# A graph layer's attention scores on VectorE: 16 multiply-and-add operations per sub-batch in place of two products and one sum

## The chip, the cores and the metric

The kernel runs on one core of one Trainium2 chip. The metric is the device time of one execution in microseconds (us); smaller is better. The kernel before takes 2039.41 us, the median of three runs (2039.25 to 2039.56).

A core has TensorE (PE, with its weight loads shown as PEld), VectorE (DVE), ScalarE (ACT), GpSimd (POOL) and SyncE (SP), which work side by side, each through its own instructions in order, and meet at semaphores.

## The reference

A graph of 6250 nodes with 256 features has 100000 edges of 5 types. Each node gets a query, a key and a value per type, each of 4 heads of 64 elements. An edge's score is the dot product of its target's query and its source's key, head by head; the scores are normalized by a softmax over the edges that share target and type, and weigh the values that are added up in the target node.

```python
q_i = Q[edge_type, dst]
k_j = K[edge_type, src]
v_j = V[edge_type, src]
score = jnp.sum(q_i * k_j, axis=-1) * scale          # per edge and head, over 64 elements
seg = dst * R + edge_type
m = jax.ops.segment_max(score, seg, num_segments=N * R)
e = jnp.exp(score - m[seg])
s = jax.ops.segment_sum(e, seg, num_segments=N * R)
alpha = e / s[seg]
out = jax.ops.segment_sum(v_j * alpha[..., None], dst, num_segments=N)
x = _layernorm(x + out.reshape(N, HD) + bias, axis=-1)
```

## The kernel before

The kernel has three stages. In the first, VectorE sorts the edges by target and type while TensorE makes queries, keys and values of all nodes, which go to tables in DRAM. The second stage walks over the sorted edges. The third adds the input, normalizes and stores. The change lies in the second stage alone.

In the second stage 128 edges form a tile (one edge per partition), 4 tiles a sub-batch (`SB = 4`), 8 sub-batches a batch of 32 tiles for which the softmax is done at once (`PERC = 8`). There are 208 sub-batches (`NSB`). All engines run a loop over the sub-batch number `s`, each with its own program, and nothing orders them but semaphores. For one sub-batch:

- GpSimd starts 4 gathers (line 468), one per tile: for each edge the row of its source's value and key (2 x 256 f32) goes from DRAM into the ring `ring_v`/`ring_k`, which has 22 places. Before a gather it waits on `s_mul` for the scores of the sub-batch 5 earlier, and on `s_agg` for the ring's place.
- SyncE loads the queries' rows of the sub-batch (line 532) and, broadcast, their places (`rel_tab`, line 525).
- TensorE (`lift`, line 709) spreads the queries to the edges with a one-hot matrix: four tiles of 128x256 into two PSUM banks, `qk`, in two halves of two tiles. Each half waits on `s_mul` until VectorE has read that half of the sub-batch before, and signals `s_lift`. Then `aggregate` (line 697) adds up the weighted values of the sub-batch 13 back.
- ScalarE scales values by their weights (line 881) and moves finished windows into the accumulator `acc` (line 899).
- VectorE runs the loop over `s` that is quoted below. `products(s, half)` (line 1210) multiplies two tiles of keys in SBUF by two tiles of queries in PSUM: 128x512 elements into `prod`. `scores(s)` (line 1216) adds up `prod` over the 64 elements of each tile and head: 128x1024 elements into 16 columns of `sc`. Around them stand four small additions of columns to the accumulator, `add_first` (line 1293, each waits for the one before through `s_acc`), the weighting of one tile of values (`payload`, line 1276), the one-hot matrix for the queries (line 1199) and four one-hot matrices for the aggregation (line 1267). In four of eight sub-batches `weights_a` and `weights_b` add a part of the softmax: running maxima and sums (lines 1220 to 1227), differences and a reciprocal (line 1259).

```python
                if s < NSB:
                    products(s, 0)
                if adds:
                    dve.wait_ge(s_cols, q - 1)
                    add_first(q - 2, 0, at)
                if s < NSB:
                    products(s, 1)
                ...
                if s < NSB:
                    scores(s)
```

Of the kernel before, what the change touches and what calls it, by code (L numbers as in the profile page):

```python
# [8 lines left out]
def gnn_kernel(nc, x, src, dst, etype, Wq, bq, Wk, bk, Wv, bv, bias, out):  # L9
    f32, i32, u16, bf16 = mybir.dt.float32, mybir.dt.int32, mybir.dt.uint16, mybir.dt.bfloat16  # L10
    ALU, ACT, AX = mybir.AluOpType, mybir.ActivationFunctionType, mybir.AxisListType
# [4 lines left out]
    H = 4  # L16
    D = C // H
# [33 lines left out]
    SB = 4  # L51
    NSB = TT // SB
    PERC = G // SB
# [92 lines left out]
    with ctx:  # L146
# [88 lines left out]
        ring_k = ring_v[:, C:C + RING].rearrange("p (i l c) -> p i l c", i=SB, l=KS)  # L235
# [5 lines left out]
        sc = cut(2 * H * G).rearrange("p (s h g) -> p s h g", s=2, h=H)  # L241
# [16 lines left out]
        prod = cut(SB * C).rearrange("p (i w) -> p i w", i=SB)  # L258
# [25 lines left out]
        qk = pairs.rearrange("p b (i w) -> p (b i) w", w=C)  # L284
# [27 lines left out]
        s_oht, s_lift, s_mul, s_sc = sem("s_oht"), sem("s_lifted"), sem("s_mul"), sem("s_sc")  # L312
# [48 lines left out]
        def spot(s):  # L361

            return KSTEP * s % KS
# [193 lines left out]
        def _(pe):  # L557
# [58 lines left out]
            for o in range(NO):  # L616
# [15 lines left out]
                for k in range(KC):  # L632
                    done = nc.tensor.matmul(bank[o % 4][0:n, 0:w], acc[:, k, t * P:t * P + n],  # L633
                                            w_sb[:, k, :, :].rearrange("p u c -> p (u c)")[:, c0:c0 + w],
                                            start=(k == 0 and o >= OA), stop=(k == KC - 1))
# [39 lines left out]
            def weights_b(s):  # L675
                c, k = piece(s)
                if k == 0:
                    pe.wait_ge(s_sc, s + 1)
                    nc.tensor.transpose(bank[6][:, 0:P], sc[:, c % 2, :, :].rearrange("p h g -> p (h g)"), ident[:]  # L679
                                        ).then_inc(s_ST, 1)  # L680
                if k == 1:
                    turn_carries(c, 0)
                if k == 2:
                    turn_rows(c, 1)
# [43 lines left out]
            for u, t in enumerate((recM, recD, recS)):  # L728
                done = nc.tensor.transpose(bank[6][0:64, u * P:(u + 1) * P], t[:].rearrange("p s c -> p (s c)"), ident[:])
            done.then_inc(s_r1, 1)  # L730
            pe.wait_ge(s_r2, 1)
            for h in range(H):
                done = nc.tensor.transpose(bank[7][0:64, h * 64:(h + 1) * 64],
                                           M4[0:64, h:h + 1].broadcast_to([64, 64]), ident[0:64, 0:64])
# [4 lines left out]
            for half in range(2):  # L739
                done = nc.tensor.transpose(bank[5][0:64, half * P:(half + 1) * P],  # L740
                                           recT[:, half, :, :].rearrange("p s c -> p (s c)"), ident[:])
# [3 lines left out]
            for half in range(2):  # L745
                done = nc.tensor.transpose(bank[6][:, half * 64:(half + 1) * 64], recV[0:64, half * P:(half + 1) * P],
                                           ident[0:64, 0:64])
# [205 lines left out]
        def _(dve):  # L953
# [21 lines left out]
                                                op0=ALU.mult, op1=ALU.add))  # L975
# [226 lines left out]
            def products(s, half):  # L1202

                if half == 0:
                    dve.wait_ge(s_got[s % KL], gathered(s))
                dve.wait_ge(s_lift, 2 * s + half + 1)
                if s > 0:
                    dve.wait_ge(s_sc, s)
                two = slice(2 * half, 2 * half + 2)
                nc.vector.tensor_tensor(prod[:, two, :], ring_k[:, two, spot(s), :], qk[:, two, :], ALU.mult  # L1210
                                        ).then_inc(s_mul, 1)

            def scores(s):
                dve.wait_ge(s_mul, 2 * s + 2)
                g = SB * (s % PERC)
                nc.vector.tensor_reduce(sc[:, (s // PERC) % 2, :, g:g + SB].rearrange("p h g -> p g h"),  # L1216
                                        prod.rearrange("p i (h d) -> p i h d", h=H), AX.X, ALU.add).then_inc(s_sc, 1)

            def scans(to, data, flags, op, start):
                c.go(nc.vector.tensor_tensor_scan(to[:, 0, :], flags[:, 0:P], data[:], start[0], op[0], op[1]))  # L1220
# [79 lines left out]
            for s in range(NSB + LAG + 2):  # L1300
                u, q = s - AHEAD, s - LAG
                adds = 0 <= q - 2 < NSB
                if adds and q % 2 == 0:
                    at = load_nodes(q - 2)
# [8 lines that stand above are left out]
                    add_first(q - 2, 1, at)  # L1313
                weights_a(s)
                if adds:
                    add_first(q - 2, 2, at)
                if s < NSB:
                    scores(s)
                if 0 <= u < NSB:
                    payload(u)  # L1320
                if s + 2 < NSB:
                    turned_one_hot(s + 2)
                if adds:
                    add_first(q - 2, 3, at)
                if 0 <= q + 1 < NSB:
                    one_hot(q + 1)
                if adds and (q - 2) % PERC == PERC - 1:
                    sum_records((q - 2) // PERC)
                weights_b(s)
# [109 lines left out]
```

## Time and profile before

| | |
|---|---|
| median of three runs | 2039.41 us |
| the profiled execution | 2043.67 us, its span 2041.9 us |
| busy over the span | PE 1692.2 us (83%), DVE 1619.3 us (79%), POOL 1152.7 us (56%), ACT 1045.8 us (51%) |
| line 1210, products | 416 instructions, 278.3 us |
| line 1216, sums of products | 208 instructions, 252.1 us |

The page's part on slices cuts the span into 40 equal pieces and gives each engine's busy share in tenths. A row of the timeline has the start of an instruction in us from the start of the span, its duration in us, the engine, line and operation, output and inputs, and in brackets how long the engine stood idle before and what ended that. Durations on VectorE overlap: an instruction's record lasts until its results are written, and the next one often starts before that. So two figures are told apart here, the record (the duration of a row) and the pitch (from a row's start to the start of the next one on the engine), and where VectorE never stands idle the pitches are what adds up to time. Rows of several instructions (x2, x4) run from the first's start to the last's end.

### The profile page before, as it was taken

The page shows a single profiled execution, that of the slowest core. Times are in us where ns is not written, and L with a number is a line of the kernel's source. Part 1 is how long each engine was busy: PE and PEld are TensorE (multiplying, and loading weights), DVE is VectorE, ACT ScalarE, POOL GpSimd, SP SyncE. Part 2 cuts the span into 40 slices and gives each one's busy share as a digit, 9 for nine tenths or more (in the row PEclk, how much of TensorE's full clock was granted, in tenths as well). Part 3 has the DMA queues.
Part 4 walks back from the last instruction along what each step waited for, and adds up shares of the span by engine and source line. Part 5 has one row for each costly group of instructions (what it writes and reads, how often), then busy time and mean ns, then how long its engine had stood idle before and what let it go on. Part 6 is the DMA issues. An engine that isn't in the chain of part 4 may idle for free.

```text
span 2041.9 us, 33205 instructions
## 1 busy us (share of the span) xinstructions
PE 1692.2 (83%) x7565; PEld 1136.7 (56%) x7565; DVE 1619.3 (79%) x4151; ACT 1045.8 (51%) x4107; POOL 1152.7 (56%) x1215
## 2 busy tenths in 40 slices
PE   5999999999999995687788877788777887788645
PEld 2444444444444443466666666666666676677534
DVE  7988897454443344799999999999999999999548
ACT  1223330200000000378888788788888888878835
POOL 2000005777777505777777777777777777776105
PEclk9999999999999997899999999999999999989668
DMA  6333344999999948999999999999999999998006
GB/s 214 124 124 109 124 141 160 313 350 364 364 362 363 339 154 292 339 318 329 320 316 320 318 333 311 320 320 321 334 309 321 320 326 329 324 306 291 24 22 210
DMA packets 339496, 555.34 MB, mean 272 GB/s; under 512 B 44045, under 2 KB 238831, under 8 KB 339298
## 3 DMA queue, kind: packets, MB, share of 16 engines
q0 software_dynamic: 80880, 256.60, 36.7%
q1 hardware_dynamic: 222180, 228.67, 34.2%
q10 hardware_dynamic: 36238, 67.94, 9.2%
q8 instruction: 61, 1.00, 0.2%
q14 instruction: 137, 1.12, 0.2%
HBM read 412.09 MB, written 140.94 MB: 271 GB/s over the span
## 4 chain that ended last, share of the span: by engine, by line
DVE 35%; PE 33%; issue 16%; POOL 8%; DMA 4%; DVEq 2%; ACT 1%; SPq 0%; ACTq 0%; POOLq 0%
PE sums L633 24%; POOL region L468 8%; DVE region L996 6%; DVE region L1267 5%; DVE region L1210 4%; PE pairs L709 4%; DVE region L1199 3%; PE sums L697 3%; DMA region<-kv_tab,kvidx 3%; DVE acc L1293 3%; DVE region L1276 2%; DVEq L1284 1%; DVE region L1221 1%; DVE region L1400 1%; DVE region L1403 1%
## 5 line engine op out<-in xcount | busy, mean ns | idle before, releaser
L468 POOL DMA_INDIRECT region<-kv_tab,kvidx x831 | 818.2, 985 | 361.1 <-issue 214.8
L881 ACT ACTIVATE region<-region 128x64 f32<-128x64 f32 x2496 | 694.1, 351 | 0.0
L633 PE MATMUL sums<-region,acc 128*128 128x512 f32 (+2 forms) x1568 | 679.5, 579 | 4.1 <-DVE region L1171 3.3
L709 PE MATMUL pairs<-region 128*128 128x256 f32 x1664 | 449.4, 416 | 181.7 <-DVE region L1210 156.4
L709 PEld LDWEIGHTS pairs<-region 128*128 128x128 f32 x1664 | 323.3, 204 | 256.6 <-issue 195.1
L697 PE MATMUL sums<-region 128*128 128x131 f32 x3328 | 438.5, 286 | 28.1 <-issue 24.5
L633 PEld LDWEIGHTS sums<-region,acc 128*128 128x128 f32 (+1 forms) x1568 | 284.8, 190 | 305.9 <-issue 290.4
L697 PEld LDWEIGHTS sums<-region 128*128 128x128 f32 x3328 | 417.1, 199 | 60.2 <-issue 52.2
L1177 DVE TENSOR_TENSOR region<-sums,region 128x512 f32<-128x512 f32 (+1 forms) x245 | 168.7, 690 | 249.9 <-PE sums L633 245.5
L450 POOL DMA_INDIRECT region<-q_tab,region x288 | 275.3, 956 | 92.8 <-issue 61.3
L899 ACT COPY acc<-sums 128x256 f32 x832 | 305.9, 368 | 30.0 <-PE sums L697 28.6
L1210 DVE TENSOR_TENSOR region<-region,pairs 128x512 f32<-128x512 f32 x416 | 278.3, 675 | 36.5 <-DMA region<-kv_tab,kvidx 24.5
L1216 DVE TENSOR_REDUCE region<-region 128x16 f32<-128x1024 f32 x208 | 252.1, 1212 | 0.8 <-issue 0.2
L868 ACT COPY region<-bank 128x128 f32<-128x128 f32 x26 | 6.9, 266 | 424.6 <-PE bank L679 423.8
L1267 DVE TENSOR_SCALAR region<-iota_f,nrel 128x131 f32<-128x131 f32 x832 | 195.1, 311 | 12.8 <-PE sums L697 12.8
L996 DVE TENSOR_TENSOR region<-region 128x512 f32<-128x512 f32 x292 | 188.9, 688 | 5.1
L787 ACT COPY region<-sums 128x512 f32<-128x512 f32 x138 | 71.1, 515 | 210.6 <-PE sums L633 210.6
L1293 DVE TENSOR_TENSOR acc<-acc,region 128x2 f32 x832 | 129.4, 156 | 30.8 <-ACT region L907 10.1
L430 POOL DMA_DIRECT2D rel_tab<-region x1 | 0.8, 768 | 245.7 <-DVE region L1113 245.7
L1199 DVE TENSOR_SCALAR region<-region,part_f 128x512 f32<-128x512 bf16 x208 | 101.6, 488 | 11.2 <-DMA region<-rel_tab 11.2
L477 POOL TENSOR_TENSOR region<-region 128x256 f32<-128x256 f32 (+1 forms) x49 | 35.4, 734 | 113.8 <-DMA region<-in_x 113.6
L1276 DVE TENSOR_TENSOR region<-region 128x256 f32<-128x256 f32 x208 | 86.4, 415 | 0.0
(246 smaller groups left out, 953.0 us busy)
## 6 DMA issues: line engine op xcount, KB each, us to landing
region<-q_seg SPq DMA_DIRECT2D x832, 128.0 KB
kv_tab<-region ACTq DMA_DIRECT2D x48, 1280.0 KB, 7.7
q_seg<-region SPq DMA_DIRECT2D x288, 128.0 KB, 5.3
q_tab<-region SPq DMA_DIRECT2D x48, 640.0 KB, 3.3
region<-rel_tab SPq DMA_DIRECT2D x208, 128.0 KB, 5.2
region<-kv_tab,kvidx POOLq DMA_INDIRECT x831
region<-in_x SPq DMA_DIRECT2D x96, 128.0 KB, 3.1
out<-region SPq DMA_DIRECT2D x48, 128.0 KB, 2.3
```

Source lines behind the costliest of these rows:

```text
L450: pool.indirect_dma_start(pq[:, j % PQ, :], None, q_tab, bass.IndirectOffsetOnAxis(ap=seg_list[:, j:j + 1], axis=0)).then_inc(s_pq[j % PQ] ...
L468: pool.indirect_dma_start(ring_row[:, a:a + 2 * C], None, kv_tab, bass.IndirectOffsetOnAxis(ap=kvidx[:, t:t + 1], axis=0)).then_inc(s_got[ ...
L633: done = nc.tensor.matmul(bank[o % 4][0:n, 0:w], acc[:, k, t * P:t * P + n], w_sb[:, k, :, :].rearrange("p u c -> p (u c)")[:, c0:c0 + w], ...
L697: done = nc.tensor.matmul(bank[i][:, h * W:(h + 1) * W], ring_v[:, i, spot(q), h * P:(h + 1) * P], oneh[:, q % 2, i, :], start=True, stop= ...
L709: done = nc.tensor.matmul(qk[:, i, :], oht[:, s % 2, i * P:(i + 1) * P], qring[:, s % QS, i, :], start=True, stop=True)
L881: done = nc.scalar.activation(ring_v[:, i, spot(q), h * D:(h + 1) * D], ring_v[:, i, spot(q), h * D:(h + 1) * D], ACT.Copy, scale=alT[:, h ...
L899: nc.scalar.copy(acc[:, :, bass.ds(at[(q % 2) * SB + i] + 1, P)], bank[i][:, 0:2 * W].rearrange("p (h n) -> p h n", h=2)[:, :, 0:P]).then_ ...
L996: nc.vector.tensor_tensor(to[:, :, half, :], one, other_half, ALU.max if half else ALU.min).then_inc(s_sort, 1)
L1210: nc.vector.tensor_tensor(prod[:, two, :], ring_k[:, two, spot(s), :], qk[:, two, :], ALU.mult).then_inc(s_mul, 1)
L1216: nc.vector.tensor_reduce(sc[:, (s // PERC) % 2, :, g:g + SB].rearrange("p h g -> p g h"), prod.rearrange("p i (h d) -> p i h d", h=H), AX ...
L1267: done = nc.vector.tensor_scalar(oneh[:, q % 2, i, :], iota_f[:, 1:W + 1], nrel[:, t:t + 1], None, ALU.is_equal)
L1293: nc.vector.tensor_tensor(acc[:, :, bass.ds(col, 1)], acc[:, :, bass.ds(col, 1)], cols[:, q % CS, i, :, 2:3], ALU.add).then_inc(s_acc, 1)
```

## The change

`products` no longer writes only products. For each of the two tiles of its half and each of the 4 heads it issues one `tensor_tensor_reduce` over 64 elements: it writes the 64 products to `prod` and their sum to one column of `sc`. That makes 8 operations per half and 16 per sub-batch. `scores` is gone, with its place in the loop and its wait. `s_mul` now comes from the last operation of each half; the wait ahead of it is on the same half of the sub-batch before. TensorE's transpose of the scores waits on `s_mul` in place of `s_sc`.

```diff
@@ -675,7 +675,7 @@
                 if k == 0:
-                    pe.wait_ge(s_sc, s + 1)
+                    pe.wait_ge(s_mul, 2 * s + 2)
                     nc.tensor.transpose(bank[6][:, 0:P], sc[:, c % 2, :, :].rearrange("p h g -> p (h g)"), ident[:]
                                         ).then_inc(s_ST, 1)
@@ -1205,16 +1205,15 @@
                 dve.wait_ge(s_lift, 2 * s + half + 1)
                 if s > 0:
-                    dve.wait_ge(s_sc, s)
-                two = slice(2 * half, 2 * half + 2)
-                nc.vector.tensor_tensor(prod[:, two, :], ring_k[:, two, spot(s), :], qk[:, two, :], ALU.mult
-                                        ).then_inc(s_mul, 1)
-
-            def scores(s):
-                dve.wait_ge(s_mul, 2 * s + 2)
+                    dve.wait_ge(s_mul, 2 * (s - 1) + half + 1)
                 g = SB * (s % PERC)
-                nc.vector.tensor_reduce(sc[:, (s // PERC) % 2, :, g:g + SB].rearrange("p h g -> p g h"),
-                                        prod.rearrange("p i (h d) -> p i h d", h=H), AX.X, ALU.add).then_inc(s_sc, 1)
+                for i in (2 * half, 2 * half + 1):
+                    for h in range(H):
+                        done = nc.vector.tensor_tensor_reduce(
+                            out=prod[:, i, h * D:(h + 1) * D], in0=ring_k[:, i, spot(s), h * D:(h + 1) * D],
+                            in1=qk[:, i, h * D:(h + 1) * D], scale=1.0, scalar=0.0, op0=ALU.mult, op1=ALU.add,
+                            accum_out=sc[:, (s // PERC) % 2, h, g + i:g + i + 1])
+                done.then_inc(s_mul, 1)
@@ -1314,8 +1313,6 @@
-                if s < NSB:
-                    scores(s)
```

## Rows read from the trace of the kernel before

**Rows 1.** Page, busy tenths in 40 slices (about 51 us each).

```profile
DVE  7988897454443344799999999999999999999548
PEclk9999999999999997899999999999999999989668
DMA  6333344999999948999999999999999999998006
```

**Rows 2.** Stretches: us, busy us of line 1210 (instructions), PEclk, DMA share, GB/s.

```profile
790.10:870.20 80.10, 20.77 (x32) 0.85 1.02 350
870.20:1891.70 1021.50, 257.50 (x384) 0.95 0.96 319
```

**Rows 3.** The second stretch, busy us: PE, PEld, DVE, ACT, POOL; then PEclk, DMA share, GB/s.

```profile
870.20:1891.70 1021.50, 811.69 (x4920) 692.32 (x4920) 982.71 (x2969) 833.84 (x3473) 749.23 (x761) 0.95 0.96 319
```

**Rows 4.** Waits of VectorE, 740 to 1900 us: us in total, times, longest.

```profile
DVE region L1210 <- DMA region<-kv_tab,kvidx: 24.5, 21, 2.3
DVE region L1210 <- PE pairs L709: 0.8, 2, 0.5
```

**Rows 5.** Timeline of VectorE, one sub-batch without softmax work.

```profile
1237.36 0.68 DVE L1210 TENSOR_TENSOR region<-region,pairs 128x512 f32<-128x512 f32 x1
1237.95 0.15 DVE L1293 TENSOR_TENSOR acc<-acc,region 128x2 f32 x1
1238.03 0.68 DVE L1210 TENSOR_TENSOR region<-region,pairs 128x512 f32<-128x512 f32 x1
1238.62 0.45 DVE L1293 TENSOR_TENSOR acc<-acc,region 128x2 f32 x2
1238.98 1.21 DVE L1216 TENSOR_REDUCE region<-region 128x16 f32<-128x1024 f32 x1
1240.11 0.41 DVE L1276 TENSOR_TENSOR region<-region 128x256 f32<-128x256 f32 x1
1240.44 0.48 DVE L1199 TENSOR_SCALAR region<-region,part_f 128x512 f32<-128x512 bf16 x1
...
1241.70 0.68 DVE L1210 TENSOR_TENSOR region<-region,pairs 128x512 f32<-128x512 f32 x1
```

**Rows 6.** Timeline of VectorE: small operations, far from the scores.

```profile
3.78 0.11 DVE L963 MEMSET recM<- 128x64 f32 x1
3.85 0.11 DVE L964 MEMSET recD<- 128x64 f32 x1
...
1966.29 0.21 DVE L1368 TENSOR_TENSOR region<-bank,region 128x50 f32<-128x50 f32 x1
1966.42 0.20 DVE L1369 TENSOR_TENSOR region<-bank,region 128x50 f32<-128x50 f32 x1
```

**Rows 7.** Timeline of VectorE: running sums over 128 elements.

```profile
1218.03 0.40 DVE L1226 TENSOR_TENSOR_SCAN region<-region 1x128 f32<-1x128 f32 x1
1218.35 0.39 DVE L1227 TENSOR_TENSOR_SCAN region<-region 1x128 f32<-1x128 f32 x1
1218.67 0.65 DVE L1210 TENSOR_TENSOR region<-region,pairs 128x512 f32<-128x512 f32 x1
```

**Rows 8.** Timeline of VectorE in the first sub-batches.

```profile
814.29 1.28 DVE L1210 TENSOR_TENSOR region<-region,pairs 128x512 f32<-128x512 f32 x2 [2.03 <-DMA region<-kv_tab,kvidx]
819.35 1.28 DVE L1210 TENSOR_TENSOR region<-region,pairs 128x512 f32<-128x512 f32 x2 [2.13 <-DMA region<-kv_tab,kvidx]
```

**Rows 9.** Timeline of TensorE: usual, after a long pause, and after the last scores.

```profile
1251.66 1.97 PE L709 MATMUL pairs<-region 128*128 128x256 f32 x8 [0.68 <-DVE region L1210]
1253.47 1.96 PE L697 MATMUL sums<-region 128*128 128x131 f32 x16
...
1786.99 3.31 PE L709 MATMUL pairs<-region 128*128 128x256 f32 x8 [3.71 <-DVE region L1210]
...
1925.88 3.83 PE L697 MATMUL sums<-region 128*128 128x131 f32 x16 [0.68 <-issue]
```

## The prediction

> **What bounds the kernel now.** The page's slices come first: from the 18th slice to the 37th VectorE is busy nine tenths or more, and before and behind that it isn't [rows 1]. That is the stage over the edges, and the change touches nothing else. The DMA row stands at nine tenths as well, so the second question is whether VectorE or the transfers set the pace. The table of stretches answers it. I cut the stage where the waits for gathers end. From 790.1 to 870.2 us there are 32 products, so 16 sub-batches, in 80.1 us: 5.01 us each, at 350 GB/s. From 870.2 to 1891.7 us there are 384 products, 192 sub-batches, in 1021.5 us: 5.32 us each, at 319 GB/s [rows 2]. In the second stretch VectorE's records sum to 982.7 us of 1021.5, TensorE's to 811.7, ScalarE's to 833.8 and GpSimd's to 749.2 [rows 3]. The table of waits says the same: over the whole stage the products waited 24.5 us for gathered rows and 0.8 us for TensorE [rows 4], and the timeline puts most of the former into the first sub-batches, with gaps of 2.03 and 2.13 us ahead of the products [rows 8]. So 192 sub-batches go at VectorE's pace, where a microsecond more on VectorE is a microsecond of the kernel, and 16 go at the transfers' pace, where VectorE has some 2 us to spare. A faster VectorE would soon meet the transfers: 5.01 us against 5.32 leaves 0.31 us per sub-batch, 60 us in all.
>
> **What is removed.** VectorE is in order and never idle here, so I take pitches (start to next start), not records. The first product starts at 1237.36 and the next instruction at 1237.95: 0.59 us. The second runs from 1238.03 to 1238.62, again 0.59 us. The sum runs from 1238.98 to 1240.11: 1.13 us [rows 5]. Removed are 2.31 us per sub-batch. The records (0.68, 0.68 and 1.21) would give 2.57, of which 0.26 us lies under the following instructions and was never on the path.
>
> **What is added: the multiply pass.** 16 operations on 128x64, keys from SBUF and queries from PSUM like the product now. The trace has no such operation. Three pitches of two-input operations bound it: 0.59 us for 512 elements, 0.33 us for 256 (1240.11 to 1240.44) [rows 5], and 0.13 us for 50 elements, which also reads PSUM [rows 6]. The line through the first two is 1.016 ns per element and 0.07 us fixed, which puts 50 elements at 0.12 us (seen: 0.13) and 64 elements at 0.135; from the 50 elements upwards 64 come to 0.145. The addition's row has the same fixed part: 128x2 elements from 1237.95 to 1238.03, 0.08 us, almost nothing but start-up. I take 0.14 us. That the fixed part is paid 16 times and no longer three times is the whole matter: 16 x 0.14 = 2.24 us, just under the 2.31 removed, before a single sum has been written.
>
> **What is added: handing out the sum.** Each operation has a second output, one column. No row shows that, so it has bounds. From below: nothing, since the present sum hands out its 16 columns within 1.13 us for 1024 elements, or even a trifle less than nothing if the column comes with the last product. In between: a further small instruction in the queue, without a wait, 0.07 us or so, like the 128x2 addition's 0.08 [rows 5] or the 128x64 memset's 0.07, which reads nothing [rows 6]. From above: a small operation that may only start when the one before has finished, as the two additions behind the second product, of which the second waits for the first; the pair takes 0.36 us to the next start [rows 5], so the first of them some 0.29. I take 0.07 us: the sum of a stream is known only when its last element has passed, and it goes to another address than the products, which is nearer to one more small instruction than to nothing; and it needs no semaphore, so it is nearer to the plain addition than to the waiting one. The Trainium skill (VectorE: DVE Perf Modes, section on two Vector instructions with no wait between them) says that an operation which also writes out its accumulator is two instructions, the main one and a read of the accumulator, and that each is held back only if its start quadrants differ from those before. Here all start at partition 0. No row here can confirm that; it would agree with a second term and with its small value, so with 2241 us; without the second term the same working gives 2.24 us against 2.31 and 2026 us.
>
> **The sum.** Per sub-batch 16 x (0.14 + 0.07) = 3.36 us added, 2.31 removed: 1.05 us more, 6.37 us in place of 5.32. Over 192 sub-batches that is 202 us. The first 16 sub-batches gain 16.8 us of VectorE work, against the gaps of some 2 us each [rows 8] that the 24.5 us [rows 4] are mostly made of; I cost them at nothing, and at most 17 us if the cover fails in those with softmax work. The profiled execution took 2043.7 us with a span of 2041.9, 4.3 us over the median of the runs; nothing outside the stage changes, so I put the 202 us on the median, 2039.4 + 202 = 2241 us; a profiled execution would be some 4 us above.
>
> **Waits and order.** The wait on the same half of the sub-batch before is satisfied a whole loop ago: nothing. What is queued behind it is all of VectorE's loop, but it doesn't stop there. Dropping the wait of the sum on its own products gains nothing, since two additions lie between. TensorE's transpose of the scores is released by the last product, at the same place or earlier: nothing. `lift` gets its half of PSUM free only when all 8 operations have read it, some 1.7 us after their start and not 0.59. Behind the second half's release TensorE has half a lift (about 1 us) and the aggregation (1.96 us) to do [rows 9], 3 us. The next release comes 3.6 us after the second product's end: 3.08 us from there to the next product now (1238.62 to 1241.70), less the sum's 1.13 [rows 5], and 1.7 for the first half's operations. So it keeps up, and the lift is done well before the products ask for it. GpSimd's gathers wait on `s_mul` five sub-batches back and have 5.01 us of work per 6.37: they stand waiting more often, with the ring full. ScalarE has 833.8/192 = 4.3 us of work per sub-batch. No other engine becomes the bound.
>
> **Rivals.** (1) The sum comes free and the fixed part shrinks: if a 64-element operation costs what its elements and 0.06 us need, 0.13 us, and the column nothing, the sub-batch costs 2.08 us against 2.31 and the kernel gets 0.23 x 192 = 44 us faster, 1995 us; the transfers would allow that (0.31 us). The point from which this decides is 2.31/16 = 0.144 us per operation with all that belongs to it. For it speaks the sum's row, whose columns cost nothing visible; against it the 0.13 us that even 50 elements take [rows 6]. 0.1 for this side, and 0.04 for within 0.2% around the break-even. (2) A cheap read, 0.02 to 0.05 us, as it has no input to fetch: 2.56 to 3.04 us, 50 to 140 us slower, 2090 to 2180 us; 0.12. (3) The sum has to wait until the pass is through, or the pass itself runs at half pace. The first adds the part by which a record outlasts its pitch (0.68 - 0.59 = 0.09 us); the second is what the running sums show, which feed each result into the next element: 128 elements at a pitch of 0.32 us [rows 7], so 2 ns per element and 0.06 fixed, and 0.07 us more for 64. Either gives about 0.29 us per operation, 4.6 us per sub-batch, 2.3 us more, 440 us, 2480 us. The scan is the only row of an operation with feedback, but the present sum also feeds back and goes at one element per 1.1 ns; 0.22. (4) The pass and its sum each wait until the other is written: a record of 0.22 us (0.14 + the 0.08 to 0.09 of overlap) and one of 0.15 like the addition's [rows 5], 0.37 us at least, 5.9 us per sub-batch, 3.6 more, 2730 us and up; 0.06. (5) TensorE's clock. After a pause of 3.71 us the lift took 3.31 us and not 1.97, and in the tail the aggregation stays at 3.83 us with pauses of 0.68 [rows 9], the granted clock being at 0.6 there [rows 1], so much of it at 1.2 GHz. With pauses a microsecond longer it may fall more often; a whole sub-batch at 1.2 GHz is 3.31 + 3.83 = 7.1 us of TensorE, over VectorE's 6.37. Were it always so, 0.77 x 192 = 150 us more, 2390 us; but an engine that never pauses doesn't stay at the low clock, as the 1.97 us show; 0.04.
>
> **How the numbers follow.** The forecast case, 0.19 to 0.25 us per operation, has 0.42: 3.04 to 4.0 us per sub-batch, 2180 to 2365 us, with 2241 us as its value. Range: it must leave out no more than 0.2. Case 4 and the two cases at and below the break-even are 0.06 + 0.1 + 0.04 = 0.2 and stay out, the others are in: 2090 to 2500 us. A measurement of this kernel can tell 0.2%, 4 us, from no change. Faster 0.1, within 0.04, slower 0.86.
>
> **What would show it.** In the profile after, line 1210's place holds 3328 operations of 128x64 whose records are near 0.22 us and whose pitch is near 0.21, perhaps with as many tiny ones of their own; the stretch between the first sub-batches and the last product grows by about 200 us with VectorE still at nine tenths, the first 16 sub-batches stay at 5.0 us each, the DMA share falls to about 0.8 and GpSimd waits more for the products. A pitch under 0.144 us, a VectorE with idle time ahead of the products, or a lift that the products wait for would prove me wrong.

## The result, and the profile after

The changed kernel takes 2050.74 us, the median of four runs (2050.09 to 2055.87), against 2039.33 us for the kernel before beside it. The ratio is 1.006, with a 95% interval of 1.0046 to 1.0075: 11 us slower, where 202 us slower was forecast. The profiled execution took 2055.9 us, the slowest of the four, with a span of 2054.0; that of the kernel before took 2043.7, so the two traces lie 12.2 us apart. Where one execution took far longer than the others of its kernel (four in the study, 2275 to 9238 us), the ratios leave it out and the medians keep it, which moves none of them by more than 1.3 us.

The page after, its busy times and the two rows of its slices that answer to [rows 1]:

```profile
PE 1724.4 (84%) x7565; PEld 1129.6 (55%) x7565; DVE 1614.7 (79%) x10183; ACT 1041.8 (51%) x4107; POOL 1154.0 (56%) x1215
...
DVE  7988897454444444799999999999999999999648
...
DMA  7333344999999949999999999999999999999006
```

VectorE issues 6032 instructions more (10183 against 4151) and is busy 4.6 us less. The DMA row didn't sink either. The same cut of the stage as in [rows 2] and [rows 3], with the first 16 sub-batches and the other 192 (columns: stretch, its length, busy us of PE, PEld, DVE, ACT, POOL, PEclk, DMA share, GB/s):

```profile
790.70:872.00 81.30, 52.50 (x176) 36.78 (x176) 56.52 (x572) 16.56 (x67) 61.81 (x65) 0.75 1.00 338
872.00:1905.60 1033.60, 846.90 (x4938) 690.96 (x4936) 979.06 (x8534) 830.39 (x3469) 749.14 (x759) 0.94 0.95 316
```

The first stretch grew by 1.2 us, the second by 12.1 us: 5.38 us per sub-batch against 5.32. So the loss lies in the stage that was named, but it is 0.06 us per sub-batch and not 1.05. The timeline of VectorE shows why, with the two halves of one sub-batch (columns as in [rows 5]):

```profile
1239.45 0.22 DVE L1212 CUSTOM_DVE_ANT_0 region<-region,pairs 128x64 f32<-128x64 f32 x1 [0.50 <-issue]
...
1240.59 0.16 DVE L1292 TENSOR_TENSOR acc<-acc,region 128x2 f32 x1
1240.68 0.22 DVE L1212 CUSTOM_DVE_ANT_0 region<-region,pairs 128x64 f32<-128x64 f32 x1
1240.83 0.08 DVE L1212 DVE_READ_ACCUMULATOR2_ANT region<- 128x1 f32 x1
1240.83 0.22 DVE L1212 CUSTOM_DVE_ANT_0 region<-region,pairs 128x64 f32<-128x64 f32 x1
1240.97 0.08 DVE L1212 DVE_READ_ACCUMULATOR2_ANT region<- 128x1 f32 x1
...
1241.82 0.17 DVE L1292 TENSOR_TENSOR acc<-acc,region 128x2 f32 x1
```

Each operation has two records, as expected: the pass and a read of the accumulator. But the next pass starts at the same moment as the read (1240.83 both). Eight operations take 1240.59 - 1239.45 = 1.14 us, and the other eight 1241.82 - 1240.68, 1.14 us again: 0.142 us each, and 2.28 us for 16. Removed were 2.31 us. The forecast's break-even stood at 0.144.

I then summed all pitches of VectorE by line, less the idle time in brackets, over the same 184 sub-batches of both traces (the 19th to the 202nd). Products and sums took 2.319 us per sub-batch before and 2.276 after; with small shifts of other lines VectorE's work went from 5.242 to 5.233 us. Its idle time went from 0.091 to 0.169 us. So the change made VectorE's work smaller by 0.01 us and its waiting longer by 0.08, some 14 us in all. Gathered rows make 10 us of that; 2 us are waits that nothing in the profile ended ("issue", 12.9 us in 30 waits against 10.7 in 23), and the rest are single waits for other engines. The table of waits names the kind, over the whole stage of the changed kernel (columns: who waited for what, us in total, times, longest), to be read against [rows 4]:

```profile
DVE region L1212 <- DMA region<-kv_tab,kvidx: 33.1, 28, 3.2
```

33.1 us for gathered rows against 24.5. Behind 870 us, where the first sub-batches are through, it is 15.1 us in 18 waits against 5.8 in 9:

```profile
DVE region L1212 <- DMA region<-kv_tab,kvidx: 15.1, 18, 1.4
```

```profile
DVE region L1210 <- DMA region<-kv_tab,kvidx: 5.8, 9, 1.5
```

The first of these two is the changed kernel from 870 to 1905 us, the second the kernel before from 870 to 1892. Numbered by their remainder by 8, the reciprocal stands at the end of sub-batch 2. The 18 waits come at most once in each round of the softmax (8 sub-batches, some 43 us), and always at one of two neighbouring places: 2.8 us of them fall ahead of the products of sub-batch 7 and 12.3 us ahead of those of the sub-batch 0 that follows, and in the kernel before 1.7 and 4.2 us. That is the distance of the ring: the gather of sub-batch 7 waits for the aggregation that TensorE does in its turn 3, behind the lift that had to wait for the reciprocal.

### The profile page after: what moved, and what is told of

Read it like the earlier page. It is cut to its first block, busy times and chain, and to the rows that moved or that the text cites. A ratio compares the mean times of both kernels' runs of the same rounds, so it can differ in the third digit from the quotient of the medians.

```text
span 2054.0 us, 39237 instructions
## 1 busy us (share of the span) xinstructions
PE 1724.4 (84%) x7565; PEld 1129.6 (55%) x7565; DVE 1614.7 (79%) x10183; ACT 1041.8 (51%) x4107; POOL 1154.0 (56%) x1215
## 4 chain that ended last, share of the span: by engine, by line
DVE 38%; PE 31%; POOL 11%; issue 10%; DMA 8%; DVEq 1%; ACT 0%; SPq 0%; ACTq 0%; POOLq 0%
PE sums L633 24%; DVE region L1212 12%; POOL region L468 11%; DMA region<-kv_tab,kvidx 7%; DVE region L996 6%; DVE region L1266 4%; PE sums L697 2%; PE pairs L709 2%; DVE acc L1292 2%; DVE region L1199 2%; DVE region L1220 1%; DVE region L1219 1%; DVE region L1397 1%; DVE region L1400 1%; DVE region L1258 1%
## 5 line engine op out<-in xcount | busy, mean ns | idle before, releaser
L709 PE MATMUL pairs<-region 128*128 128x256 f32 x1664 | 489.2, 429 | 200.4 <-DVE region L1212 179.6
L1212 DVE CUSTOM_DVE_ANT_0 region<-region,pairs 128x64 f32<-128x64 f32 x3328 | 499.9, 213 | 48.7 <-DMA region<-kv_tab,kvidx 33.1
L709 PEld LDWEIGHTS pairs<-region 128*128 128x128 f32 x1664 | 318.2, 208 | 317.9 <-issue 215.5
L1212 DVE DVE_READ_ACCUMULATOR2_ANT region<- 128x1 f32 x3328 | 262.5, 79 | 0.6 <-issue 0.3
```

What stands on the lines that cost most here:

```text
L709: done = nc.tensor.matmul(qk[:, i, :], oht[:, s % 2, i * P:(i + 1) * P], qring[:, s % QS, i, :], start=True, stop=True)
L1212: done = nc.vector.tensor_tensor_reduce(out=prod[:, i, h * D:(h + 1) * D], in0=ring_k[:, i, spot(s), h * D:(h + 1) * D], in1=qk[:, i, h * ...
```

## The experiments

Four questions: what an operation of 64 elements costs, what its sum costs, where the extra waits come from, and what less work on VectorE would be worth. Some runs came on two chips on which the kernel before takes 2357.7 and 2350.2 us, not 2041. They were repeated elsewhere, and conclusions for this case rest on the repeats; both are given. Every time below is a median, beside that of the kernel before on the same chip.

### What an operation costs, and its sum

Three kernels keep the old sum (`scores`) and cut the products into 16 operations: plain products, then the multiply-and-add operation without its column, then with it.

```diff
-                two = slice(2 * half, 2 * half + 2)
-                nc.vector.tensor_tensor(prod[:, two, :], ring_k[:, two, spot(s), :], qk[:, two, :], ALU.mult
-                                        ).then_inc(s_mul, 1)
+                for i in (2 * half, 2 * half + 1):
+                    for h in range(H):
+                        done = nc.vector.tensor_tensor(
+                            prod[:, i, h * D:(h + 1) * D], ring_k[:, i, spot(s), h * D:(h + 1) * D],
+                            qk[:, i, h * D:(h + 1) * D], ALU.mult)
+                done.then_inc(s_mul, 1)
```

That is e1; here and below, "..." stands for lines left out of a diff. In e2 the operation is the changed kernel's `tensor_tensor_reduce` with `accum_out=None`, in e3 with its column of `sc`.

> The kernel before with its two products of 128x512 cut into 16 plain products of 128x64; the sum over the 64 elements stays as it was. The theory that a small operation costs 0.142 us whatever it hands out, and that the sum's hand-out is free: pitch 0.14 us, 16 x 0.142 - 1.19 = 1.08 us more per sub-batch, about 2240 us. The rival that the multiply-and-add operation has a cheaper start than a plain product, which pays for its hand-out: a plain pitch above 0.15 us, over 2270 us.

> The kernel before with 16 multiply-and-add operations of 128x64 that hand out no sum (products alone are written), and the old sum behind them. If the hand-out is free: the same as with the column, about 2240 us, one record per operation, pitch 0.142 us. If the hand-out costs part of the 0.142 us: pitch down to 0.13 or less, 2200 us or less.

> The kernel before with 16 multiply-and-add operations of 128x64 that hand out their sums to sc, and the old sum behind them, which writes the same columns again. If the hand-out is free: equal to the run without the column within 5 us, about 2240 us. If it costs 0.07 us as predicted: 1.1 us per sub-batch above the run without the column, 215 us.

On the first chip, with 2357.7 us before: 2394.8, 2390.1 and 2510.9 us. Only 37 us of the 175 expected for the plain pieces showed there. That other waits in the stage covered the rest is my reading; the kernel before wasn't traced on that chip. The pitches could be read all the same, and the repeats were forecast from them.

> The kernel before with 16 plain products of 128x64 and the old sum, once more on another chip. From the pitch of 0.131 us that the first profile shows: 16 x 0.131 - 1.19 = 0.91 us more per sub-batch, 175 us over 192 sub-batches, 2215 us. Were the pitch 0.142 as with the column: 2245 us.

> 16 multiply-and-add operations that hand out no sum, and the old sum, once more on another chip. If the multiply-and-add pass costs what a plain product costs: equal to the run with plain pieces within 3 us, 2215 us, pitch 0.131 us.

> The same with the sums handed out, and the old sum behind them, once more on another chip. If handing out a sum costs the 0.011 us between the pitches 0.142 and 0.131: 16 x 0.011 = 0.18 us per sub-batch, 34 us over the run without the column, 2250 us. If the 3328 further instructions cost time besides their pitch, as the 120 us on the first chip suggest: 50 us or more over it, with idle time ahead of the operations that no engine's signal ends.

With 2040.8 us before: 2211.1, 2211.1 and 2250.7 us (two executions each). The timelines of VectorE, first with plain pieces, then with the fused operation without its column:

```profile
1304.32 1.14 DVE L1211 TENSOR_TENSOR region<-region,pairs 128x64 f32<-128x64 f32 x8
1305.37 0.16 DVE L1296 TENSOR_TENSOR acc<-acc,region 128x2 f32 x1
```

```profile
1303.95 1.12 DVE L1212 CUSTOM_DVE_ANT_0 region<-region,pairs 128x64 f32<-128x64 f32 x8
1305.00 0.15 DVE L1298 TENSOR_TENSOR acc<-acc,region 128x2 f32 x1
```

Both take 1.05 us for eight, 0.131 us each. With the column, in the third kernel:

```profile
1304.46 0.22 DVE L1212 CUSTOM_DVE_ANT_0 region<-region,pairs 128x64 f32<-128x64 f32 x1 [0.50 <-issue]
1304.60 0.08 DVE L1212 DVE_READ_ACCUMULATOR2_ANT region<- 128x1 f32 x1
1304.60 0.22 DVE L1212 CUSTOM_DVE_ANT_0 region<-region,pairs 128x64 f32<-128x64 f32 x1
...
1305.60 0.08 DVE L1212 DVE_READ_ACCUMULATOR2_ANT region<- 128x1 f32 x1
```

Eight take 1305.60 - 1304.46 = 1.14 us, 0.142 each. So multiplying and adding in one pass costs what multiplying costs, and handing out the sum costs 0.011 us, a sixth of what I took. Time agrees: 39.6 us over the run without the column, where 16 x 0.011 x 208 = 37 us. Against before, 16 x 0.131 - 1.19 = 0.91 us more per sub-batch gave 170 us, where 175 was expected. Here a microsecond more on VectorE is a microsecond of the kernel.

The size of the fixed part was tested with pieces of 32 elements:

```diff
-                    for h in range(H):
+                    for j in range(2 * H):
+                        a = slice(32 * j, 32 * (j + 1))
...
                         done = nc.vector.tensor_tensor_reduce(
-                            out=prod[:, i, h * D:(h + 1) * D], in0=ring_k[:, i, spot(s), h * D:(h + 1) * D],
+                            out=ring_k[:, i, spot(s), a], in0=ring_k[:, i, spot(s), a],
...
```

Of each head's two sums only one goes to `sc`, the other to a place in `prod` that nobody reads, so half of each dot product is left out.

> The changed kernel with 32 operations of 32 elements per sub-batch, in place, where only one of the two sums of each head goes to sc, so half of each dot product is left out. If an operation costs its elements and 0.075 us and the hand-out is hidden: pitch 0.108 us, 3.46 us per sub-batch, 1.2 us more than the changed kernel, 2280 us. If the hand-out has a price of its own that the 64 elements covered: pitch 0.14 us, 4.5 us, 2480 us.

Measured: 2320.7 us, 2041.0 before.

```profile
1299.96 0.18 DVE L1214 CUSTOM_DVE_ANT_0 region<-region,pairs 128x32 f32<-128x32 f32 x1
1300.07 0.08 DVE L1214 DVE_READ_ACCUMULATOR2_ANT region<- 128x1 f32 x1
1300.07 0.18 DVE L1214 CUSTOM_DVE_ANT_0 region<-region,pairs 128x32 f32<-128x32 f32 x1
...
1300.83 0.08 DVE L1214 DVE_READ_ACCUMULATOR2_ANT region<- 128x1 f32 x1
```

Eight operations from 1299.96 to 1300.83 are 0.109 us each. From 32 to 64 elements that is 0.033 us for 32 elements, so 1.04 ns per element and 0.075 us fixed, the handed-out sum in it. The kernel is 40 us slower than expected from that pitch over 192 sub-batches. Half of it goes if all 208 are counted (1.2 us each for the first 16); the other half stays open.

### Where the waits for gathered rows come from

The ring holds 22 sub-batches' rows, and a gather must wait until the values 17 sub-batches back are aggregated. TensorE does that aggregation behind the lift, and the lift behind VectorE's products. I tested the ring first. In the changed kernel nobody reads `prod`, so the products can be written over the keys, and the 1024 words of `prod` give the ring a 23rd place.

```diff
-                            out=prod[:, i, h * D:(h + 1) * D], in0=ring_k[:, i, spot(s), h * D:(h + 1) * D],
+                            out=ring_k[:, i, spot(s), h * D:(h + 1) * D], in0=ring_k[:, i, spot(s), h * D:(h + 1) * D],
```

That is e5, the control. e4 adds

```diff
-    KS = 22
+    KS = 23
...
-        prod = cut(SB * C).rearrange("p (i w) -> p i w", i=SB)
```

> The changed kernel with its products written over the keys in the ring, not to prod; all else as in the changed kernel. Every theory: the same as the changed kernel, 2050 us within 3. It is the control for the next.

> The same, and the room of prod given to the ring, which gets 23 places in place of 22, so that a gather waits for an aggregation one sub-batch older. If the late release of the ring's place makes the extra idle time: VectorE's waits for gathered rows behind the first sub-batches fall from 15 us to under 5, the kernel takes 2033 to 2042 us. If the number of instructions or the transfers themselves make it: 2048 to 2052 us.

The kernel before can have the same ring, if its gathers wait for the sum (`s_sc`), as the products now lie where the keys were:

```diff
-                    pool.wait_ge(s_mul, 2 * (s - KL + 1))
+                    pool.wait_ge(s_sc, s - KL + 1)
...
-                nc.vector.tensor_tensor(prod[:, two, :], ring_k[:, two, spot(s), :], qk[:, two, :], ALU.mult
+                nc.vector.tensor_tensor(ring_k[:, two, spot(s), :], ring_k[:, two, spot(s), :], qk[:, two, :], ALU.mult
...
```

> The kernel before with its products written over the keys and 23 places in the ring (the gather then waits for the sum of the sub-batch 5 earlier, not its products). The late-release theory: the 6 us of waits for gathered rows mostly go, 2033 to 2037 us, as VectorE's work per sub-batch is the same to 0.02 us. The rival: no change, 2037 to 2041 us.

With 2040.96 us before: in place 2051.2 us (ratio 1.0050, 1.0035 to 1.0065), ring of 23 with the change 2036.7 us (0.9976, 0.9966 to 0.9987), ring of 23 without it 2037.0 us (0.9981, 0.9969 to 0.9993). VectorE's waits in the changed kernel with 23 places, from 870 to 1885 us:

```profile
DVE region L1211 <- issue: 13.1, 30, 0.5
DVE region L1224 <- ACT region L834: 3.7, 3, 2.0
DVE region L1274 <- issue: 0.7, 3, 0.2
DVE region L1211 <- DMA region<-kv_tab,kvidx: 0.6, 1, 0.6
```

The waits for gathered rows are gone, and with them 14.5 us of the changed kernel and 4 us of the one before. The two kernels come out equal, within 0.3 us. For the one before, 2037.0 us lies on the border of its two expectations, with the interval of its ratio wholly below 1. So the loss of the change runs through the ring's place; with one place more, its 6032 further instructions cost nothing that the medians show. Their trace shows a little: 13.1 us in 30 waits that nothing in the profile ended, where the kernel before with 23 places has 11.1 us in 24. Both beat the kernel before, and no kernel of the study that does the whole computation is faster.

What delays the ring's place was less plain. The changed kernel frees PSUM later: the first half 1.14 us after the first product's start and the second after 2.37, where it was 0.59 and 1.26. First I delayed the second half alone, in the kernel before:

```diff
                 if s < NSB:
                     products(s, 0)
...
+                if 0 <= u < NSB:
+                    payload(u)
+                if s + 2 < NSB:
+                    turned_one_hot(s + 2)
                 if s < NSB:
                     products(s, 1)
```

with the same four lines taken away behind `scores`.

> The kernel before with the weighting of one tile (0.33 us) and the queries' one-hot (0.40 us) moved from behind the scores to between the two products; the same instructions, but the second product ends 0.73 us later after the first. If the changed kernel lost its time because the second half of PSUM comes free later in the sub-batch (TensorE's lift and aggregation, the ring's place, the gathers): about two thirds of that loss, 7 to 10 us slower, with more idle time of VectorE for gathered rows. If it lost it to the number of instructions or to chance: within 2 us of before.

On the first chip 2387.6 us against 2357.7, 1.012, which looked like a confirmation. On the second:

> The kernel before with the weighting of one tile and the queries' one-hot moved to between the two products, once more, on another chip than the one whose kernel before took 2358 us. Late release of the second half of PSUM as the cause of the changed kernel's loss: 7 to 10 us slower than before, VectorE's waits for gathered rows behind the first 16 sub-batches up from 5.8 us to 10 or more. Number of instructions or chance: within 2 us of before, those waits unchanged.

2041.4 us against 2040.8 (1.0004, 0.9990 to 1.0018), and 1.5 us of waits for gathered rows. The second half alone isn't it, and on this point my theory fell. TensorE's timeline in the changed kernel shows which release may matter, with the lift behind the longest pause of the batch:

```profile
1240.82 3.52 PE L709 MATMUL pairs<-region 128*128 128x256 f32 x8 [3.61 <-DVE region L1212]
```

and in the kernel before:

```profile
1233.83 3.13 PE L709 MATMUL pairs<-region 128*128 128x256 f32 x8 [3.62 <-DVE region L1210]
```

After 3.6 us of pause these lifts run for 3.1 to 3.5 us and not 1.97 [rows 9]. The granted clock over them is 0.55 in the changed kernel and 0.60 in the one before, so most of either runs at 1.2 GHz and not 2.4; over the lifts of 1.90 us that follow it is 1.00. They start when the first half is free. My theory now was that a second half that comes 0.73 us later finds TensorE still at the first. The trace of e6b doesn't bear that out:

```profile
1232.57 1.11 PE L709 MATMUL pairs<-region 128*128 128x256 f32 x4 [3.39 <-DVE region L1210]
1233.88 2.07 PE L709 MATMUL pairs<-region 128*128 128x256 f32 x4 [0.20 <-DVE region L1210]
```

TensorE is through with the first half and waits 0.20 us for the second. The delay reaches the lift, and costs nothing all the same. The next two kernels delayed the first half, by one wait of TensorE: in e12 in the kernel before, in e13 in that of e6.

```diff
-                        pe.wait_ge(s_mul, 2 * (s - 1) + half + 1)
+                        pe.wait_ge(s_mul, 2 * s)
```

> The kernel before, with one wait of TensorE changed: the lift of the first half waits for both products of the sub-batch before and not only for the first, so it starts some 0.67 us later; VectorE's program is the same. If the later release of the first half makes the changed kernel's loss (the lift after the long pause ends later, then the aggregation, the ring's place and the gather): 5 to 12 us slower than before, waits for gathered rows behind the first 16 sub-batches up from 5.8 us to 10 to 18. If the release has no part in it: within 2 us of before.

> The same wait of TensorE, in the kernel whose second product stands 0.73 us later: the lift of both halves starts some 2.0 us after the start of the first product, and not 0.6; in the changed kernel the halves are free after 1.14 and 2.37 us. If the release makes the loss: at least that of the run with only the first half late, 10 to 20 us slower than before. If it has no part: within 2 us of before.

These met the other of the two slower chips: 2370.1 and 2455.0 us against 2350.2. The repeats:

> The kernel before, with the lift of the first half waiting for both products of the sub-batch before, once more on another chip. If the later release of the first half makes the changed kernel's loss: 5 to 12 us slower than before, waits for gathered rows behind the first 16 sub-batches up from 5.8 us to 10 to 18. If it has no part: within 2 us of before.

> The lift waiting for both products, and the second product 0.73 us later, once more on another chip. If the release makes the loss: 10 to 20 us slower than before, and more than the run with only the first half late. If it has no part: within 2 us of before.

2050.6 us (1.0043, 1.0030 to 1.0056) and 2086.8 us (1.0221, 1.0207 to 1.0236), with 2040.7 before. The second is far over the 10 to 20 us expected: its lifts behind the reciprocal start 2.24 us after the first product's start, where the changed kernel's do so after 1.40 (means of the table below). In the first, with VectorE's program untouched, a first half that comes 0.67 us later costs 10 us, as much as the change. But the other half of the expectation failed. VectorE's waits in e12b from 870 to 1885 us:

```profile
DVE region L1210 <- DMA region<-kv_tab,kvidx: 6.1, 11, 1.1
DVE region L1220 <- ACT region L839: 4.1, 9, 0.7
```

6.1 us for gathered rows is what the kernel before has (5.8). There are new waits of 4.1 us for the softmax's carries, which TensorE turns behind the lift and ScalarE moves (line 839), and the rest of the 10 us lies in pitches that are a little longer (5.267 us of work per sub-batch against 5.242). In e13b the waits for ScalarE and the carries come to 28 us and those for gathered rows to 2.5.

What the traces show of the chain is how far the turn behind the reciprocal shifts. The table has means over 22 such turns (first products of sub-batches 19, 27 ... 187), in us from that first product's start: when the lift starts, how long it takes and at what granted clock, when the aggregation of that turn ends, and when the first gather of the sub-batch four later starts.

| kernel | lift starts | takes | clock | aggregation ends | gather starts | ratio |
|---|---|---|---|---|---|---|
| before | 0.83 | 2.90 | 0.72 | 6.03 | 6.48 | 1 |
| second half late (e6b) | 0.84 | 3.33 | 0.64 | 6.58 | 6.89 | 1.0004 |
| first half late (e12b) | 1.50 | 2.96 | 0.70 | 6.70 | 6.98 | 1.0043 |
| both halves late (e13b) | 2.24 | 3.02 | 0.65 | 7.85 | 8.12 | 1.0221 |
| changed | 1.40 | 3.49 | 0.59 | 7.45 | 7.72 | 1.006 |
| before, 23 places | 0.83 | 2.74 | 0.75 | 5.89 | 0.90 | 0.9981 |
| changed, 23 places | 1.40 | 3.53 | 0.56 | 7.39 | 1.85 | 0.9976 |

In the changed kernel the gather starts 1.24 us later than before. The lift starts 0.57 us later and takes 0.59 us longer, at a lower granted clock. With 23 places the lift and the aggregation are as late, but the gather no longer stands behind them. So the chain from the late halves to the late gather is there in the trace, and the experiment with the ring shows that the gather's wait for its place makes the loss. What no edit isolated is which of the two halves makes it, and why the lift takes longer. The run with the first half late seems to lose its 10 us in another way: its gather is hardly later than that of e6b (6.98 and 6.89 us), which lost nothing. That it loses as much as the change is then no proof for the chain. The waits for gathered rows vary from execution to execution as well: 15.1 us in the changed kernel's profile, 8.0 us in that of e5, which has the same program but for the place of the products.

### What less work on VectorE would be worth

```diff
-                    for h in range(H):
+                    for j in range(2):
```

where each operation takes elements 128j to 128j + 127, so two heads at once, and its sum goes to column 2j of `sc`. The sums of single heads are left out, so this isn't the whole computation; it tells what 0.6 us less work on VectorE is worth.

> The changed kernel with 8 operations of 128 elements per sub-batch, each over two heads at once; the sums of single heads are left out. Pitch 0.133 + 0.075 = 0.21 us, 1.68 us per sub-batch in place of 2.27, so 0.6 us less work for VectorE. If the transfers end that gain at 5.01 us per sub-batch as the first 16 show: 0.39 us less per sub-batch, about 1975 us, and VectorE waits for gathered rows for 40 us or more. If they can follow faster: 1935 us.

2328.4 us against 2350.2 on the second of the slower chips, and repeated:

> The changed kernel with 8 operations of 128 elements per sub-batch, each over two heads at once (the sums of single heads are left out), once more on another chip. Pitch 0.21 us, 0.6 us less work for VectorE per sub-batch. If the transfers end the gain at 5.01 us per sub-batch: about 1975 us, with VectorE waiting for gathered rows for 40 us or more. If they can follow faster: 1935 us.

2015.1 us against 2040.7. The row of stretches from 900 to 1800 us (columns: as above), and VectorE's waits for gathered rows from 870 to 1885:

```profile
900.00:1800.00 900.00, 732.72 (x4466) 618.16 (x4465) 784.54 (x4932) 751.21 (x3142) 688.55 (x693) 0.96 0.98 330
```

```profile
DVE region L1212 <- DMA region<-kv_tab,kvidx: 85.1, 77, 2.8
```

VectorE's work fell to 4.65 us per sub-batch, yet a sub-batch takes 5.20 us, and VectorE waits 85 us for rows. The 2015.1 us lie above both times expected, 1975 and 1935 us. With a DMA share of 0.98, and GpSimd waiting for the ring's place for only 25.4 us from 870 to 1885, I read 5.20 us as the transfers' pace in the middle of the stage, not the 5.01 us of the first sub-batches; no run separates the transfers from the other engines there. The kernel before, at 5.32 to 5.33, was 0.13 us over it. That would be why so small a shift makes waits: there is next to no reserve in which the gathers could catch up after the long sub-batch.

## Why the prediction was wrong, point by point

**What bounds the stage: right, with one number wrong.** VectorE sets the pace, and 0.91 us of work per sub-batch cost 170 us. But I read the transfers' pace from the first 16 sub-batches, where neither aggregation nor payloads run, and got 5.01 us. By e9b it is 5.20, and the reserve 0.13 us and not 0.31.

**What is removed: right.** 2.31 us by pitches; 2.32 as a mean over 184 sub-batches. Records instead of pitches would have given 2.57.

**The pass: 0.14 us taken, 0.131 measured,** for the plain product and the fused one alike. The 0.145 from the 50-element row was too high, the line through 256 and 512 elements with 0.135 near.

**Handing out the sum: the step that failed.** I took 0.07 us, a small instruction of its own, and it is 0.011. The second instruction is there, with a record of 0.08 us, but the next pass starts with it. My argument was that the sum needs its last element and an address of its own, "nearer to one more small instruction than to nothing". That argues for a record, not for a pitch. The memset in [rows 6] fetches nothing, and its 0.07 us is about what 64 elements alone take at the 1.016 ns of the line, with no fixed part; for one element that is next to nothing. I had this row and drew from it the 0.07 of its 64 elements. Rival (2), a cheap read "as it has no input to fetch", had the right reason, a chance of 0.12 and a price of 0.02 to 0.05 us, still too high. The Trainium skill (VectorE: DVE Perf Modes, section on two Vector instructions with no wait between them) says that the two are two instructions, held back only if start quadrants differ. The trace agrees as far as it goes: there are two records each, and no holding back with all of them at partition 0; what other start quadrants would do, these rows can't show. I set the sum's second term from the row of an addition that fetches two operands and that of a memset of 64 elements.

**The sum.** 16 x 0.142 = 2.27 us and not 3.36; the 1.05 us per sub-batch become -0.04, and the 202 us become a gain of 8 for the products and sums alone. The case "within 0.2% around the break-even" had a pitch of 0.144 and a chance of 0.04, and it described VectorE's side. The interval of the ratio lies beyond it on the slow side (1.0046 to 1.0075), through a path that I had costed at nothing.

**Waits and order: the second step that failed.** I saw that PSUM's halves would come free later and that TensorE would keep up, with 3 us of work in 3.6. That is true of the common sub-batch. The one behind the reciprocal, where TensorE pauses for 3.6 us and then runs mostly at 1.2 GHz, wasn't worked through, nor the chain from there over aggregation and the ring's place to a gather due four sub-batches later, with transfers that have 0.13 us per sub-batch to catch up. The clock stood among the rivals as a bound of TensorE as a whole, which it didn't become; it had its part in the lift behind the pause, with 0.59 granted and not 0.72.

**The first 16 sub-batches: right in the main.** 81.3 us after 80.1.

**What was to be seen in the profile.** 3328 records near 0.22 us were there (0.213 in the mean), with as many small ones; the pitch wasn't 0.21, and so the DMA share didn't fall to 0.8 but stayed at 0.95, from 0.96. GpSimd's waits for the aggregation rose from 55.1 to 68.0 us over the stage, those for the products fell from 14.3 to 11.5.

**The rivals.** That the column costs nothing was nearly so, but the pass is 0.131 us and not the 0.127 that elements and 0.06 us would give, and with 0.011 for the column nothing is left of the 44 us. Half pace, waiting for the pass, and mutual waiting didn't occur.

## What to carry to other kernels

Price an instruction by what it holds back, its pitch: the read that fetches no operands and writes one element cost a hundredth of a microsecond here, with a record of 0.08 us. Cutting a stream of 512 elements into pieces of 64 cost 0.06 to 0.075 us for each, and fusing product and sum pays only while that is less than the pass it saves: here 13 further start-ups and 16 columns weighed just as much as 1024 elements of summing. When work on the bounding engine stays the same but its milestones move, follow each milestone through the longest turn of the loop, not the common one, and look at how much reserve the next resource has; here one more place in a ring, paid for by a buffer that the fusion had made idle, was worth more than the fusion.

## What was not expected of the hardware

The read of the accumulator starts together with the next pass, and has a record of 0.08 us and a cost of 0.011 us of pitch.

The chips differ. On two of them the kernel before takes 2357.7 and 2350.2 us, 15% more. Traces of e1 and e12 there show 263 and 267 GB/s in the middle of the stage over the edges (1200 to 1900 us), where the kernel before has 316 here. On the first of the two the 3328 reads of the accumulator cost 121 us (2510.9 against 2390.1) and not 39.6. In that execution VectorE stood idle 53 us ahead of the operations and 40 us ahead of the reads with nothing in the profile that ended it:

```profile
L1212 DVE CUSTOM_DVE_ANT_0 region<-region,pairs 128x64 f32<-128x64 f32 x3328 | 511.1, 214 | 56.5 <-issue 53.3
L1212 DVE DVE_READ_ACCUMULATOR2_ANT region<- 128x1 f32 x3328 | 266.3, 80 | 41.6 <-issue 40.0
```

The same idle time was 33 us in e2 there, which has no reads, and 12 us in e3b. A slow supply of instructions would look like this, but no run tested it. What holds on one chip for the effect of a change needn't hold on another: delaying the second half cost 1.2% there and nothing here (1.0004).
